# First layer's attention scores: from three 32-row products to two, with the mask row brought in by transfer

## What is computed

```python
q = Wq @ x + bq;  k = Wk @ kv + bk;  v = Wv @ kv + bv      # per batch, 256 x 512
attn = softmax(where(kv_mask, (q / 4) . k, -inf))           # per head, 512 x 512
mean = attn @ v
std  = sqrt(relu(attn @ (v * v) - mean * mean))
out  = (masked_instance_norm(x) * std + mean) * mask
```

## Time and profile before

| | us |
|---|---|
| median of three runs | 4405.9 |
| span of the profiled execution (its own time, first to last instruction) | 4404.7 |
| PE busy | 4165.1 (95%) |
| DVE busy | 2982.4 (68%) |
| ACT busy | 1964.2 (45%) |
| first layer's work within the span | about 0 to 829 |

### The profile page before, as it was taken

How to read it: one execution, slowest core, us unless ns; L and a number is a source line. 1 busy time by engine, 2 the same in 40 slices (tenths; PEclk the granted TensorE clock), 3 DMA queues, 4 the chain that set the end, 5 groups by cost and what they waited for, 6 DMA issues and landing times. The chain is left out here.

```text
span 4404.7 us, 70578 instructions
## 1 busy us (share of the span) xinstructions
PE 4165.1 (95%) x22060; PEld 3143.8 (71%) x22060; DVE 2982.4 (68%) x6501; ACT 1964.2 (45%) x3814; POOL 1591.1 (36%) x1094
## 2 busy tenths in 40 slices
PE   7999999778999997799999999999999999999999
PEld 3444444356777775588887797887887877988866
DVE  5666666268888887475775775767766757757743
ACT  2555555322333331355553455553555543555522
POOL 1223233145566563133234323234332234332230
PEclk7999999889999999899999999999999999999999
DMA  1000000300000000222112322222222122231122
GB/s 40 26 20 30 20 20 11 125 5 11 15 15 15 16 10 15 90 63 83 58 60 74 103 63 73 64 72 72 92 65 71 58 70 99 63 96 56 54 78 98
DMA packets 128413, 239.26 MB, mean 54 GB/s; under 512 B 16933, under 2 KB 40101, under 8 KB 126897
## 3 DMA queue, kind: packets, MB, share of 16 engines
q1 hardware_dynamic: 126544, 232.46, 16.5%
q0 software_dynamic: 1008, 3.67, 0.2%
q10 hardware_dynamic: 624, 0.18, 0.0%
HBM read 220.27 MB, written 15.73 MB: 54 GB/s over the span
## 5 line engine op out<-in xcount | busy, mean ns | idle before, releaser
L2105 POOL TENSOR_TENSOR c_wl<-c_wr,c_wh 128x512 fp32r<-128x512 f32 (+1 forms) x576 | 822.0, 1439 | 1646.0 <-ACT c_wh L2472 1388.7
L2573 ACT ACTIVATE c_pr<-c_ps,c_nms 128x257 f32<-128x257 f32 x512 | 244.2, 477 | 485.1 <-DVE c_nms L2795 483.1
L582 ACT ACTIVATE a_ex<-a_ps 128x1024 f32<-128x1024 f32 x256 | 261.1, 1023 | 259.7 <-PE a_ps L417 259.7
L1629 DVE TENSOR_TENSOR_SCAN b_sb<-b_wt,b_s,b_ps 128x256 f32<-128x256 f32 x512 | 361.6, 735 | 15.6 <-PE b_ps L1082 3.2
L695 DVE TENSOR_REDUCE a_nm<-a_ps 128x2 f32<-128x1024 f32 x256 | 311.4, 1221 | 80.5 <-PE a_ps L394 80.3
L2472 ACT ACTIVATE c_wh<-c_wr 128x512 fp32r<-128x512 f32 (+1 forms) x464 | 315.3, 687 | 45.4 <-PE c_ps L2192 41.6
L1580 POOL TENSOR_TENSOR b_sb<-b_sb,b_rt 128x1024 f32<-128x1024 f32 x128 | 277.9, 2178 | 156.5 <-DVE b_sb L1629 113.9
L2190 PE MATMUL c_ps<-c_hh,c_wh 128*128 128x512 f32 x768 | 309.1, 402 | 12.9 <-DVE c_hl L2679 12.6
L2190 PE MATMUL c_ps<-c_gh,c_wh 128*128 128x512 f32 x768 | 307.7, 401 | 5.6 <-DVE c_gl L2857 2.9
L2192 PE MATMUL c_ps<-c_hh,c_wl 128*128 128x512 f32 x768 | 304.4, 396 | 0.0
L2191 PE MATMUL c_ps<-c_hl,c_wh 128*128 128x512 f32 x768 | 303.8, 396 | 0.0
(11 more groups left out here) (379 smaller groups left out, 10578.6 us busy)
## 6 DMA issues: line engine op xcount, KB each, us to landing
c_wr<-in_downs SPq DMA_DIRECT2D x192, 256.0 KB, 2.7
c_wr<-in_wv SPq DMA_DIRECT2D x64, 512.0 KB, 3.9
c_wr<-in_wk SPq DMA_DIRECT2D x128, 256.0 KB, 2.9
c_wr<-in_wq SPq DMA_DIRECT2D x128, 256.0 KB, 2.6
c_wr<-in_fc SPq DMA_DIRECT2D x64, 256.0 KB, 2.8
b_w<-in_w SPq DMA_DIRECT2D x8, 1024.0 KB, 14.7
a_x<-in_x SPq DMA_DIRECT2D x8, 512.0 KB, 3.9
a_ctx<-in_ctx SPq DMA_DIRECT2D x8, 512.0 KB, 4.4
```

Source lines behind the costliest of these rows:

```text
L582: act.activation(EX[:, n % 4, :, :], ps[:, BT + 2 * (n % 2):BT + 2 * (n % 2) + 2, :], ACT.Exp).then_inc(ex_ready, 1)
L1629: mm = dve.tensor_tensor_scan(SB[:, quad % RING, pr % 2, e, 1:L + 1], WT[:, third(b, i), e, :], half(spread_bank(pair), e), S0[:, b % 2, 2 ...
L2105: pool.tensor_tensor(piece(WL, slot), piece(WR, slot), piece(WH, slot), ALU.subtract).then_inc(piece_cut[slot], 1)
L2573: act.activation(PR[:, i, 0:L + 1], ps[:, BS + 1 - i % 2, 0:L + 1], ACT.Exp, bias=NMS[:, i:i + 1], scale=float(K2) ** -0.5, accum_out=RS[: ...
```

## The change

The 16 unused rows of each head are filled with a second copy of the channels. Weights and biases are loaded doubled (rows 0 to 15 and 16 to 31 alike). Per-row factors `FIRST` (1 in rows 0 to 15), `SECOND` (1 in rows 16 to 31), `ADD_Q` (2^-20 at row 16) and `ADD_K` (1 at row 17) then make:

- `QH`, `KH`: as before, high parts in rows 0 to 15, mask and maximum rows after them. ACT's instruction gets a per-partition scale beside the bias.
- `QL`: the rest of the queries in rows 0 to 15, the queries themselves in rows 16 to 31.
- `KL`: the keys themselves in rows 0 to 15, the rest of them in rows 16 to 31. For it ACT writes one more tile, `KM` (128 x 512), ahead of `KH`, and DVE subtracts `KM` where it subtracted `KH`.

So `KL.QL` is both corrections in one product, and scores are two products a head. The mask value becomes -2^120, its unit in the queries 2^-20. The seventh product of the key projection is gone; SP instead writes the mask row from `MBRR` into row 16 of `KH` by four transfers of one row of 2 KB each, after `KH` is written, and PE's maxima wait for these. DVE makes the mask row in group 1 (steps 2 and 3) instead of group 0 (steps 5 and 6) and counts valid positions in step 4 instead of step 1.

```diff
-NEG = -1e30
+NEG = -(2.0 ** 120)
@@ SP
+            def place_mask(b, g):
+                sp.wait_ge(mask_ready, b + 1 + AHEAD)
+                sp.sem_inc(passed, 1)
+                sp.wait_ge(kh_ready, b * G0 + g + 1 + AHEAD)
+                sp.sem_inc(passed, 1)
+                for h in range(HG):
+                    sp.dma_start(KH[32 * h + ROW_MASK:32 * h + ROW_MASK + 1, g, :].bitcast(F32), MBRR[h:h + 1, :].bitcast(F32)).then_inc(mask_in[g], 16)
             load_statistics(0)
+            place_mask(0, 0)
+            place_mask(0, 1)
+            place_mask(0, 2)
             place_maxima(0, 0)
             load_inputs(1)
             place_maxima(0, 1)
+            place_mask(0, 3)
             with sp.Fori(0, B - 2) as b:
                 place_maxima(b, 2)
+                place_mask(b + 1, 0)
                 place_maxima(b, 3)
+                place_mask(b + 1, 1)
                 load_statistics(b + 1)
                 place_maxima(b + 1, 0)
+                place_mask(b + 1, 2)
                 load_inputs(b + 2)
                 place_maxima(b + 1, 1)
+                place_mask(b + 1, 3)
@@ PE
-                pe.matmul(ps[:, BX, :], MSELR[:, :], MBRR[:, :], start=False, stop=True).then_inc(k_ps, 1)
+                mm.then_inc(k_ps, 1)
-                    pe.wait_ge(kh_ready, it + 1 + AHEAD)
+                    pe.wait_ge(mask_in[g], (b + 1) * N_HEADS + AHEAD)
-                for i, (keys, queries) in enumerate(((KH, QH), (KH, QL), (KL, QH))):
+                for i, (keys, queries) in enumerate(((KH, QH), (KL, QL))):
@@ ACT
-                act.activation(QH[:, g, :], ps[:, BX, :], ACT.Identity, bias=QKB[:, 0, g:g + 1]).then_inc(qh_ready, 1)
+                act.activation(QH[:, g, :], ps[:, BX, :], ACT.Identity, scale=FIRST, bias=HALF_B[:, 0, g:g + 1]).then_inc(qh_ready, 1)
-                act.activation(KH[:, g, :], ps[:, BX, :], ACT.Identity, bias=QKB[:, 1, g:g + 1]).then_inc(kh_ready, 1)
+                act.activation(KM[:, :], ps[:, BX, :], ACT.Identity, scale=SECOND, bias=SECOND_B[:, g:g + 1])
+                act.activation(KH[:, g, :], ps[:, BX, :], ACT.Identity, scale=FIRST, bias=HALF_B[:, 1, g:g + 1]).then_inc(kh_ready, 1)
@@ DVE
-                    dve.wait_ge(k_ps, b * G0 + AHEAD)
+                    for placed in mask_in:
+                        dve.wait_ge(placed, b * N_HEADS + AHEAD)
-                dve.scalar_tensor_tensor(KL[:, g, :], ps[:, BX, :], QKB[:, 1, g:g + 1], KH[:, g, :], ALU.add, ALU.subtract).then_inc(kl_ready, 1)
+                dve.scalar_tensor_tensor(KL[:, g, :], ps[:, BX, :], BOTH_B[:, 1, g:g + 1], KM[:, :], ALU.add, ALU.subtract).then_inc(kl_ready, 1)
-                    if g == 0 and n == 5 and more:
+                    if g == 1 and left > 2 and n == 2:
                         mask_rows(b + 1, 0)
-                    if g == 0 and n == 6 and more:
+                    if g == 1 and left > 2 and n == 3:
                         mask_rows(b + 1, 1)
-                    if g == 1 and left > 2 and n == 1:
+                    if g == 1 and left > 2 and n == 4:
                         count_valid(b + 1)
```

More of the change, by code:

```diff
@@ L24 @@
 ROW_MASK, ROW_MAX = D0, D0 + 1
+MASK_UNIT = 2.0 ** -20
 V2C = 2 * D0
 VCOLS = 64
-NEG = -1e30
+NEG = -(2.0 ** 120)
 F32 = mybir.dt.float32
@@ L47, in start_ahead, with layer0 @@
         eng.sem_inc(semaphore, AHEAD)
-def layer0(nc, x, xT, ctx, mask_row, mask_col, wqk, qkb, aug, wv, bv, mask_sel, ident_in, x1T):
+def layer0(nc, x, xT, ctx, mask_row, mask_col, wqk, qkb, aug, wv, bv, ident_in, x1T):
     with ExitStack() as stack:
@@ L78, in layer0 @@
         QKB = sb("qkb", [P, 2, G0])
-        AUG = sb("aug", [P, 2, G0])
+        AUG = sb("aug", [P, 4])
+        HALF_B = sb("half_b", [P, 2, G0])
+        BOTH_B = sb("both_b", [P, 2, G0])
+        SECOND_B = sb("second_b", [P, G0])
+        KM = sb("km", [P, E], F32R)
         BVB = sb("bvb", [P, L])
-        MSEL = sb("msel", [P, P])
-        MSELR = sb("mselr", [P, P], F32R)
         M8R = sb("m8r", [P, E], U8)
@@ L121, in layer0 @@
         BT, BM, BO, BX = 0, 4, 6, 7
+        FIRST, SECOND, ADD_Q, ADD_K = (AUG[:, i:i + 1] for i in range(4))
+        mask_in = [sem("mask_in%d" % g) for g in range(G0)]
         consts_in, inputs_in, stats_x_in, memset_done, inputs_read, mask_read, stats_read = [sem(n) for n in ("consts_in", "inputs_in", "stats_x_in", "memset_done", "inputs_read", "mask_read", "stats_read")]
@@ L178, in place_maxima @@
                                  NMT[h * EC:(h + 1) * EC, g % 2, :].bitcast(F32)).then_inc(max_in, 16)
+            def place_mask(b, g):
[5 more added lines that the diff above has]
+                    sp.dma_start(KH[32 * h + ROW_MASK:32 * h + ROW_MASK + 1, g, :].bitcast(F32), MBRR[h:h + 1, :].bitcast(F32)).then_inc(mask_in[g], 16)
             sp.dma_start(WQK, wqk).then_inc(wqk_in, 16)
             load_inputs(0)
-            for dst, src in ((QKB[:, :, :], qkb), (AUG[:, :, :], aug), (MSEL[:, :], mask_sel), (WV, wv), (BVB[:, :], bv),
-                             (ID[:, :], ident_in)):
+            for dst, src in ((QKB[:, :, :], qkb), (AUG[:, :], aug), (WV, wv), (BVB[:, :], bv), (ID[:, :], ident_in)):
                 sp.dma_start(dst, src).then_inc(consts_in, 16)
             load_statistics(0)
+            place_mask(0, 0)
+            place_mask(0, 1)
+            place_mask(0, 2)
             place_maxima(0, 0)
@@ L188, in _ @@
             place_maxima(0, 1)
+            place_mask(0, 3)
             with sp.Fori(0, B - 2) as b:
                 place_maxima(b, 2)
+                place_mask(b + 1, 0)
                 place_maxima(b, 3)
+                place_mask(b + 1, 1)
                 load_statistics(b + 1)
                 place_maxima(b + 1, 0)
+                place_mask(b + 1, 2)
                 load_inputs(b + 2)
                 place_maxima(b + 1, 1)
+                place_mask(b + 1, 3)
             place_maxima(B - 2, 2)
+            place_mask(B - 1, 0)
             place_maxima(B - 2, 3)
+            place_mask(B - 1, 1)
             load_statistics(B - 1)
-            for g in range(G0):
-                place_maxima(B - 1, g)
+            place_maxima(B - 1, 0)
+            place_mask(B - 1, 2)
+            place_maxima(B - 1, 1)
+            place_mask(B - 1, 3)
+            place_maxima(B - 1, 2)
+            place_maxima(B - 1, 3)
             sp.wait_ge(out_ready, B + AHEAD)
@@ L356, in project_keys @@
                     pe.matmul(ps[:, BX, :], WH[:, g, k, 1, :], CL[:, k, :], start=False, stop=False)
-                    pe.matmul(ps[:, BX, :], WL[:, g, k, 1, :], CH[:, k, :], start=False, stop=False)
-                pe.matmul(ps[:, BX, :], MSELR[:, :], MBRR[:, :], start=False, stop=True).then_inc(k_ps, 1)
+                    mm = pe.matmul(ps[:, BX, :], WL[:, g, k, 1, :], CH[:, k, :], start=False, stop=(k == LC - 1))
+                mm.then_inc(k_ps, 1)
             def values(b, half):
@@ L413, in scores @@
                 cols = slice(k * P, (k + 1) * P)
-                for i, (keys, queries) in enumerate(((KH, QH), (KH, QL), (KL, QH))):
+                for i, (keys, queries) in enumerate(((KH, QH), (KL, QL))):
                     for a in range(2):
                         rows = head_rows(p, a)
-                        mm = pe.matmul(ps[:, BT + 2 * (n % 2) + a, :], keys[rows, g, cols], queries[rows, g, :], start=(i == 0), stop=(i == 2))
+                        mm = pe.matmul(ps[:, BT + 2 * (n % 2) + a, :], keys[rows, g, cols], queries[rows, g, :], start=(i == 0), stop=(i == 1))
                 mm.then_inc(t_ps, 1)
@@ L673, in _ @@
             dve.tensor_tensor(XL[:, :, :], X[:, :, :], XH[:, :, :], ALU.subtract).then_inc(x_low, 1)
-            dve.wait_ge(consts_in, 6 * 16 + AHEAD)
-            dve.tensor_tensor(QKB[:, :, :], QKB[:, :, :], AUG[:, :, :], ALU.add)
+            dve.wait_ge(consts_in, 5 * 16 + AHEAD)
+            dve.tensor_scalar(QKB[:, 0, :], QKB[:, 0, :], float(D0) ** -0.5, None, ALU.mult)
             dve.drain()
-            dve.tensor_scalar(QKB[:, 0, :], QKB[:, 0, :], float(D0) ** -0.5, None, ALU.mult)
-            dve.tensor_copy(MSELR[:, :], MSEL[:, :])
+            dve.tensor_scalar(HALF_B[:, 0, :], QKB[:, 0, :], FIRST, ADD_Q, ALU.mult, ALU.add)
+            dve.tensor_scalar(HALF_B[:, 1, :], QKB[:, 1, :], FIRST, ADD_K, ALU.mult, ALU.add)
+            dve.tensor_scalar(BOTH_B[:, 0, :], QKB[:, 0, :], ADD_Q, None, ALU.add)
+            dve.tensor_copy(BOTH_B[:, 1, :], QKB[:, 1, :])
+            dve.tensor_scalar(SECOND_B[:, :], QKB[:, 1, :], SECOND, None, ALU.mult)
             dve.drain().then_inc(weights_split, 1)
@@ L3104, in pad @@
     def pad(W):
[L3105 removed]
+        z=np.stack([W.reshape(4,4,16,256)]*2,axis=2)
         return z.reshape(4,128,2,128).transpose(3,0,2,1)
     def padb(b):
[L3108 removed]
+        return np.stack([b.reshape(4,4,16)]*2,axis=2).reshape(4,128).T
     wqk=f(np.stack([pad(I['L0_xattn_Wq']),pad(I['L0_xattn_Wk'])],axis=3))
```

(1 more changed line is left out.)

7 lines of the change are left out of this document (3 added, 4 removed).

## The result

Four runs of the changed kernel gave 4419.19, 4425.44, 4428.51 and 4430.2 us; the median is 4426.98, against 4406.14 for the kernel before. The ratio is 1.0043, with an interval of 1.0029 to 1.0057: 0.43% slower, where 0.7% faster was forecast. The profiled execution took 4419.19 us with a span of 4417.5 and is the fastest of the four; the other three, of which no trace was kept, have spans of 4423.8 to 4428.6 at a mean granted clock of 0.967 to 0.969 (0.969 in the profiled one).

The account below looks back on a forecast made before the run. PE was taken to bound the kernel, busy 98.7 of 100 us in the first layer. 65.6 us gained less 36.0 of stalls is 29.6 net, giving 4376.3 us (0.7% faster), range 4350 to 4392.

Parts of the forecast that it names:

- Where this stall lands, group by group: First layer: list of PE waits caused by the longer key-work chain, each priced at its length; together 36.0 us lost.
- Group 1 also gets the count of valid positions: Group 1, step 4: the count behind `KL` delays the same reduction by 0.66 us, x 7 = 4.6 us.
- The gain on PE: First layer: 285 product pairs removed at a pitch of 0.23 us each save 65.6 us.
- Rival 1: The stalls at step 6 do not come, so nearly the whole gain stays: 4342 us; chance 0.15.
- Rival 2: Steps end by something other than PE, such as the reduction loop: within 0.2% of 4406 us; chance 0.06.
- The stall of step 6: PE waits 1.06 us ahead of step 6's maxima for DVE's reduction; 15 groups, 15.9 us.
- The scale operand: A per-partition scale beside the bias brings ACT's 128x512 activation from 0.69 to 0.78 us.
- Group 0: Batches 1 to 7: roots hold PE 0.47 us longer, 0.69 us of removed pairs bring nothing; 7 x 1.16 = 8.1 us.
- The mask by transfer: Four 2 KB transfers behind `KH` land before the next group's step 0; hidden, 0.1 to 2.5 us to spare.
- rival 4: Mask row lands late and PE waits at step 0 of each of 28 groups: slower, 4432 us; chance 0.08.
- The mask on DVE: Making the mask row in group 1, steps 2 and 3, costs 0, covered by over 1.5 us each.
- rival 3: POOL holds DVE's mask halves in group 1 and PE waits: 4398 us, or 4387 for half; chance 0.14.

Follow-up runs that it names:

- e1: Changed kernel with DVE's count of valid positions back after step 1 of group 1; 4381.25 us, ratio 0.9941.
- e2: Kernel before, with the count moved to step 4 of group 1 behind two added unused DVE reductions; 4479.36 us, ratio 1.0171.
- e8: Changed kernel with PE doing the weighted product ahead of the maxima in step 6 of groups 1 and 2; 4373.87 us, ratio 0.9915.
- e6: e5 with ACT's square roots of group 0 one step later, behind the exponential of step 6; 4358.72 us, ratio 0.9883.
- e2b: Kernel before, with only the count of valid positions moved to step 4 of group 1; 4413.47 us, ratio 1.0024, median of 13 runs.
- e3: Changed kernel with the added `KM` activation writing 32 of 512 columns within the groups; 4377.97 us, ratio 0.9941.
- e5: Changed kernel, count after step 1, `KL` behind step 5's reduction in groups 1 and 2; 4363.21 us, median of five runs (a sixth took 10183).

## Why the prediction was wrong, point by point

**The failed step** is the one that made the sum: "Where this stall lands, group by group", and in it "Group 1 also gets the count of valid positions". Each stall was priced at its length; the clock at which PE would run behind it was not a term, and the 1.00 of the earlier trace rows was carried over without a reason. Group 1's stall, seen in kind, cost 7 x 1.77 us idle and 33.7 us of lower clock in four batches. No rival had it either: the one for a slower kernel was about a transfer. e1, e2 and e8 show it from three sides.

**The gain on PE** was right: PE's own rows keep their pitch, and a batch at full clock takes 93.4 us, although it has stalls that the batch of before had not. e6 brings back 44.7 us of span.

**Rival 1** (no stalls) is out; the stalls came. **Rival 2** (no effect) is out by the 93.4 us. **The stall of step 6** was right. It shows as 0.89 us idle, but the pitch tells its price: from 376.25 to 377.54 it is 1.29 us, where undisturbed rows have 0.23, so the maxima product is 1.06 late, as forecast. The weighted product behind it comes after 0.43 us, where the step before has 0.33 (374.58 to 374.91), which makes 1.16 in all. **The scale operand** was forecast at 0.78 and measures 778 and 768 ns over 32 each:

```profile
L576 ACT ACTIVATE a_km<-a_ps,a_second_b,a_aug 128x512 fp32r<-128x512 f32 x32 | 24.9, 778 | 38.8 <-PE a_ps L383 38.8
L577 ACT ACTIVATE a_kh<-a_ps,a_half_b,a_aug 128x512 fp32r<-128x512 f32 x32 | 24.6, 768 | 0.0
```

**Sizes that were off**, with the four long falls aside (8.7 us between 4375.1 and 4383.8). They come out of the pitches of PE's rows in a batch at full clock, held against undisturbed ones, less what the kernel before loses at the same places, with what each is worth in all batches:

- Group 1, step 6: 2.04 us (1.94 late, 0.10 behind it) for 1.72, since the count delays the reduction by 0.88, its own 0.68 and 0.20 of empty time behind it: 2.2 us over seven batches.
- Step 6 elsewhere: 8 x 0.10 = 0.8 us.
- Values in group 3: 0.58 for 0.51, 0.5 us. Step 1 of group 2: it came, 0.38 for 0.24, 1.1 us.
- In no term: a wait for the values' copy in group 0, step 1 (0.37 idle, 0.43 lost, where the kernel before loses 0.22), 1.3 us; a wait of 0.30 at step 2 of group 3, where small work on DVE stands ahead of the reduction of step 1, 2.1 us.
- Group 0: the roots took 1.11 us of idle time again instead of 1.6, because the maxima's stall lies ahead of them and not inside their wait. Together they cost 1.16 + 1.17, 1.13 more than the 1.20 before, where 1.16 more was forecast: 0.2 us less.

Together 7.8 us, and 9.3 with the 1.5 of the short fall: 0.6 more than the 8.7, or 0.09 a batch, which I can't place.

**The mask by transfer** was hidden, as forecast, and rival 4 is out: it lands sooner than the 2.0 us of the earlier trace rows, and no row of PE names it as a releaser.

```profile
a_kh<-a_mbrr SPq DMA_DIRECT2D x8, 2.0 KB, 1.7
```

**The mask on DVE** was free, and rival 3 is out. A half takes 652 ns in the mean (863 before) and 1.12 us at the longest, and PE has no wait behind one:

```profile
L684 DVE TENSOR_SCALAR a_mbrr<-a_m8r 128x256 fp32r<-128x256 uint8 x16 | 10.3, 652 | 0.3 <-issue 0.3
```

**The place** was right: from the last transpose of the first layer on, the span has 3588.0 us, 3589.3 before. All of the loss lies in the first layer (829.5 us until then, 815.4 before).

**Still open:** why one wait of 1.1 to 1.8 us is followed by the lower clock and the next, equal to the rounding, is not. The same kernel differs from run to run in it (e2b), so one profile shows a draw, not the rule. Whether what PE does around the wait matters as well was not separated: the stall of 0.89 us had one fall in 61, yet the roots' 1.11, which follows it 4 us later, had one in e1 and none in the changed kernel, e3, e5 and e8; and nearly the same wait (1.13) had none in the kernel before and five in e2b.

## What to carry to other kernels

When an edit takes work from a PE that is all but full, list the waits that grow to over 1 us and price each with the clock behind it, up to 11 us here, times a chance that rises with its length. Don't put small work of another engine ahead of what releases PE, and don't join two short waits to a long one; turn PE's order so that it has a product to do meanwhile. Check the granted clock in windows of a few microseconds: the page's busy share can't tell half speed from work.

## What the runs showed of the hardware

- In a stream with PE busy in over 92% of each 100 us, 27 of 90 idle times of 1.1 to 2.3 us came with a granted clock of 0.50 for 4 to 25 us (longer only where the layer ended in it), although PE was busy at once again; of 61 idle times of 0.9 us, one did. At that clock a weighted product's row takes 1.97 us for 1.08.
- A wait of 0.89 us in the trace, ahead of a maxima product, cost 1.16 us by the pitches around it; one of 1.11 ahead of a weighted product cost 1.17.
- A count of 0.68 us on DVE holds the next reduction back by 0.88.
- An activation of 128x512 takes 598 ns plain, 688 with a bias operand and 768 to 778 with a scale operand too.
- Four transfers of one 2 KB row within SBUF take SP 2.48 us to issue, and one lands 1.7 us after its issue.
